# Rows of x and y in DRAM numbered lane by lane, two experts' KAN weights asked for on ScalarE's queue, and some normalised copies written by VectorE

## The chip, the cores and the metric

One core of one Trainium2 chip. The metric is device microseconds for one launch of the whole program. Everything is float32 in DRAM and SBUF unless it is said otherwise. SBUF has 128 partitions, called lanes below.

## The reference, cut to what matters

`x` is 2048 tokens of 128 channels. The program computes three residual steps in a row: a mixture of experts, attention with its own feed-forward part, and the same mixture again.

```python
x = x + 0.5 * ffn(layernorm(x))           # first mixture
x = x + attn(layernorm(x))                # windowed attention, then SiLU-gated ffn
x = x + 0.5 * ffn(layernorm(x))           # second mixture, the same weights

def ffn(x):                               # 8 experts, the best 2 of each token
    w_full = normalised top-2 of softmax(x @ gate_W)
    # experts 0 to 3, MLP:   gelu(x @ W1 + b1) @ W2 + b2        (128 -> 512 -> 128)
    # experts 4 to 7, KAN:   basis(layernorm(x)) @ W0 + b0, layernorm, basis, @ W1 + b1
    #   basis: 8 values 1 - tanh^2((x - grid) / 2) for each channel (1024 -> 256, 2048 -> 128)
    return sum over experts of expert_out * w_full
```

## The kernel before, in words

**Stages.** `macaron` runs `route` and `moe_blocks` for the first mixture (n = 0), then the attention (`project`, `attend`, `finish_attention`), then `route` and `moe_blocks` again (n = 1). Inside each function every engine has its own instruction stream, written by hand in the order in which it runs; there is no scheduler. Streams wait for each other only through semaphores and at the ends of the functions' blocks.

**How x lies.** `k.xs` holds token t*128 + p in lane p, tile t (16 tiles of 128 channels). In `route` two normalised copies of each token are written into `k.got`: `xn` (for the MLP experts) and `xh` (for the KAN experts), both by ScalarE, 32 activations (L560) in four chunks of four tiles. As soon as a chunk is written, the SP queue copies it to `x_rows` in DRAM (L459). There a token's row number is its token number, so one lane's four tiles of a chunk lie 128 rows apart and each goes as a run of 512 bytes.

**Routing.** TensorE transposes x (L501) and multiplies by the gate (L519); VectorE picks the best two experts, counts, and sorts the tokens into blocks of 128 with one expert each (L344 to L438). The numbers that it sorts are in `token_no`. The result is `rows_of`: for each block the rows to read from `x_rows` and the rows to write in `y_rows`. GpSimd waits until all of `x_rows` has landed (`rows_in_dram`) and until `rows_of` is ready, and then starts the first gathers (L480).

**Blocks.** `moe_blocks` gathers 128 rows by an indirect DMA of GpSimd (L692), runs the expert, and scatters the result to `y_rows` (L697). First come MLP blocks in pairs, then two blocks that fill the start of the KAN pipeline, then a joint loop that runs one MLP and one KAN block per round, and a loop for KAN blocks alone. For each MLP block ScalarE copies the expert's W1 out of `k.mlp_w1` into `m_w1` (L1173), because TensorE loads it from a fixed place; TensorE's first product waits for it (`m_w1_ready`, L849). The second product (L858) takes W2 straight from `k.mlp_w2`, hidden channel c*128 + p in lane p, slice c.

**Weights of the first mixture.** All are asked for on the SP queue, in this order: x in four parts, `b1`, W1, four W2 and b2 of the MLPs (`load_mlps`), the shared small tensors (`load_shared`), then the eight writes of `x_rows` as their chunks become ready, then eight loads of 1 MB with the KAN weights (`load_kan`, L199 and L201). `b1` comes as 16 rows that TensorE turns (L524) and ScalarE copies (L552). TensorE waits for all of the KAN weights before the first KAN product (L871).

**The end of each mixture.** When all of `y_rows` is there, they are read back into `got` in eight parts (SP for the first choice, L1255; ScalarE's queue for the second, L1243), again in runs of 512 bytes; ScalarE weighs the second (L572), VectorE adds both to x (L581, L586).

## Time and profile before

| what | value |
|---|---|
| median of 3 runs | 637.17 us (632.69 to 643.67) |
| the profiled execution, its own time | 639.1 us |
| its span from first to last instruction | 637.3 us |
| mean granted TensorE clock | 0.927 of full speed |
| TensorE busy | 558.2 us |
| VectorE, ScalarE, GpSimd busy | 454.3, 401.1, 262.1 us |
| KAN weights, first mixture | 8 loads of 1024 KB on SP's queue |

A row of a timeline tells when a group of instructions of one engine starts (microseconds from the start of the span), how long it takes from the first to the last, the line, what is written from what, and, in square brackets, how long the engine sat idle before it and what ended that. In the program the first mixture ends at about 219 us, the attention at about 420 us, and the second mixture at the end.

### The profile page before, as it was taken

What the parts mean: (1) busy time and instruction counts of PE and PEld (TensorE: products, weight loads), DVE (VectorE), ACT (ScalarE), POOL (GpSimd) and SP (SyncE); (2) the same over time, 40 slices, a digit from 0 to 9 for tenths busy, and PEclk for the clock granted to TensorE, in tenths of its full rate; (3) what the DMA queues carried; (4) which work ended last, traced back from release to release, by engine and by line L of the source; (5) the groups of instructions that cost most, each with busy time, mean ns of one, the idle gap of its engine ahead of it and who ended that gap; (6) DMA issues with size and microseconds to landing.
All of it is one profiled execution on the core that took longest, in us unless ns stands there. A gap on an engine that the chain in (4) does not pass through costs nothing. (4 is left out here: it accounts for less than half of the span.)

```text
span 637.3 us, 19397 instructions
## 1 busy us (share of the span) xinstructions
PE 558.2 (88%) x6514; PEld 494.5 (78%) x6515; DVE 454.3 (71%) x1135; ACT 401.1 (63%) x954; POOL 262.1 (41%) x314
## 2 busy tenths in 40 slices
PE   9677899999999488888889888998788999999970
PEld 8666899999999355766778783688788999999970
DVE  6734768788788576699678788557466787878864
ACT  4645868889875158710456523256587789888943
POOL 7144556555544345820000013221455556656540
PEclk7768989999999869999999999985798999999995
DMA  8793222100101220000100039303111000110106
GB/s 264 246 407 100 67 62 86 45 26 29 33 16 19 68 78 3 4 3 14 16 5 4 5 120 402 156 29 114 34 30 26 25 27 27 33 29 25 29 18 202
DMA packets 41433, 46.58 MB, mean 73 GB/s; under 512 B 7409, under 2 KB 33377, under 8 KB 40353
## 3 DMA queue, kind: packets, MB, share of 16 engines
q1 hardware_dynamic: 32272, 33.99, 15.9%
q0 software_dynamic: 4736, 9.71, 5.5%
q10 hardware_dynamic: 4368, 2.10, 1.1%
q8 instruction: 39, 0.64, 0.4%
q14 instruction: 18, 0.14, 0.1%
HBM read 35.69 MB, written 10.09 MB: 72 GB/s over the span
## 5 line engine op out<-in xcount | busy, mean ns | idle before, releaser
L881 PE MATMUL k_y_ps<-kan_w,k_basis 128*128 x1056 | 128.5, 281 | 7.3 <-DVE k_basis L978 7.3
L881 PEld LDWEIGHTS k_y_ps<-kan_w,k_basis 128*128 128x128 f32 x1056 | 124.4, 196 | 9.6 <-issue 9.2
L871 PE MATMUL k_z_ps<-kan_w,k_basis 128*128 x528 | 120.5, 381 | 0.6 <-issue 0.6
L1151 ACT ACTIVATE k_sig<-k_h1T 128x256 f32<-128x256 f32 x264 | 84.4, 402 | 47.5 <-DVE k_h1T L1005 47.4
L871 PEld LDWEIGHTS k_z_ps<-kan_w,k_basis 128*128 128x128 f32 x528 | 98.2, 191 | 13.3 <-issue 1.1
L978 DVE SCALAR_TENSOR_TENSOR k_basis<-k_sig 128x512 f32<-128x512 f32 x132 | 88.1, 690 | 14.6 <-ACT k_sig L1151 14.6
L1817 ACT ACTIVATE got<-p_ps 128x960 f32<-128x960 f32 (+1 forms) x44 | 39.2, 944 | 42.0 <-PE p_ps L1672 41.9
L1144 ACT ACTIVATE k_sig<-k_h0T 128x128 f32<-128x128 f32 x280 | 59.2, 294 | 7.6 <-DVE k_h0T L966 7.6
L697 POOL DMA_INDIRECT y_rows<-k_y,k_rows x33 | 34.3, 1041 | 53.8 <-DVE j_y L1033 28.3
L849 PE MATMUL m_z_ps<-m_xT,m_w 128*128 128x128 f32 x304 | 43.3, 289 | 8.1 <-ACT m_w L1173 4.9
L849 PEld LDWEIGHTS m_z_ps<-m_xT,m_w 128*128 128x128 f32 x304 | 41.4, 202 | 11.1 <-ACT m_w L1173 6.3
L1743 DVE TENSOR_REDUCE p_minus_max<-p_ps 128x6 f32<-128x960 f32 (+1 forms) x44 | 45.8, 1116 | 4.9 <-PE p_ps L1637 4.4
L704 POOL TENSOR_TENSOR k_rstd<-k_var_eps,minus_half 128x1 f32<-128x1 f32 x33 | 31.7, 961 | 39.8 <-DVE k_var_eps L995 39.7
L972 DVE SCALAR_TENSOR_TENSOR k_basis<-k_sig 128x512 f32<-128x512 f32 x70 | 47.8, 685 | 0.0
L1622 PE MATMUL p_ps<-s_kT,s_q_bd 32*128 32x160 f32 (+3 forms) x864 | 35.2, 303 | 8.7 <-DVE p_minus_max L1743 7.9
L858 PE MATMUL m_y_ps<-mlp_w,m_hT 128*128 x304 | 42.8, 286 | 0.0
L1622 PEld LDWEIGHTS p_ps<-s_kT,s_q_bd 32*128 32x128 f32 x864 | 30.0, 185 | 14.1 <-DVE p_minus_max L1743 13.0
L858 PEld LDWEIGHTS m_y_ps<-mlp_w,m_hT 128*128 128x128 f32 x304 | 39.0, 201 | 0.5 <-issue 0.3
L692 POOL DMA_INDIRECT k_x_in<-x_rows,k_rows x31 | 33.3, 1073 | 10.4 <-issue 8.8
L1173 ACT COPY m_w<-mlp_w 128x512 f32 x40 | 24.8, 620 | 18.0 <-issue 13.3
L1990 POOL TENSOR_TENSOR f_rstd<-f_var_eps,minus_half 128x4 f32<-128x4 f32 x4 | 5.5, 1382 | 69.9 <-DVE f_var_eps L2025 69.9
L692 POOL DMA_INDIRECT j_x_in<-x_rows,j_rows x24 | 25.1, 1046 | 20.8 <-POOL j_rows L795 16.5
(270 smaller groups left out, 1089.5 us busy)
## 6 DMA issues: line engine op xcount, KB each, us to landing
kan_w<-in_L_ffn_kan_sl_W_dram SPq DMA_DIRECT2D x16, 1024.0 KB, 14.0
x_rows<-got SPq DMA_DIRECT2D x16, 256.0 KB, 2.5
mlp_w<-in_L_ffn_mlp_W_dram SPq DMA_DIRECT2D x2, 1024.0 KB, 5.9
mlp_w<-in_L_ffn_mlp_W_dram SPq DMA_DIRECT2D x8, 256.0 KB, 6.7
got<-y_rows SPq DMA_DIRECT2D x8, 256.0 KB, 4.9
got<-y_rows ACTq DMA_DIRECT2D x8, 256.0 KB, 5.4
xs<-in_L_attn_x_dram SPq DMA_DIRECT2D x4, 256.0 KB, 3.8
s_cos<-in_cos_dram SPq DMA_DIRECT2D x8, 128.0 KB
```

The source lines that it names most:

```text
L692: pool.indirect_dma_start(dst[:], None, k.x_rows, bass.IndirectOffsetOnAxis(ap=rows.bitcast(U32), axis=0)).then_inc(landed, 16)
L849: last = nc.tensor.matmul(m_z_ps[:, c], m_w1[:, c * P:(c + 1) * P], m_xT[:], start=True, stop=True)
L858: last = nc.tensor.matmul(m_y_ps, m_hT[:, c], k.mlp_w2[:, bass.ds(e, 1), c], start=(c == 0), stop=(c == FC - 1))
L871: last = nc.tensor.matmul(z_ps, basis0[:, g], k.kan_w0[:, bass.ds(e, 1), g], start=(g == 0), stop=(g == G - 1))
L881: last = nc.tensor.matmul(y_ps, basis1[:, g, c], k.kan_w1[:, bass.ds(e, 1), c, g], start=(g == 0 and c == 0), stop=(g == G - 1 and c == F2 ...
L972: nc.vector.scalar_tensor_tensor(basis0[:, part], sig0[:, part], 1.0, sig0[:, part], ALU.subtract, ALU.mult).then_inc(basis0_ready, 1)
L978: nc.vector.scalar_tensor_tensor(basis1[:, part], sig1[:, part], 1.0, sig1[:, part], ALU.subtract, ALU.mult).then_inc(basis1_ready, 1)
L1144: ins = nc.scalar.activation(sig0[:, g], h0T[:], ACT.Sigmoid, bias=float(-GRID[g]))
L1151: ins = nc.scalar.activation(sig1[:, g], h1T[:], ACT.Sigmoid, bias=float(-GRID[g]))
L1622: nc.tensor.matmul(banks[g][:, i * SPAN + lead:(i + 1) * SPAN], s.q_bd[rows(g), b], s.kT[rows(g), b * QB + lead - WINDOW:(b + 1) * QB], st ...
L1743: nc.vector.tensor_reduce(minus_max[:, h, 2 * half:2 * half + 2, b0:b0 + n], src, AX.X, ALU.max, negate=True).then_inc(reduced, 1)
L1817: nc.scalar.activation(prob[t % 2][:, 2 * half:2 * half + 2, 0:n * SPAN], ps[:, at:end, 0:n * SPAN], ACT.Exp).then_inc(exp_done, 1)
```

## The change

Four things are changed.

1. **Numbering.** The row of a token in `x_rows` and `y_rows` is now lane*16 + tile. `token_no` is made with that number, and the views of the writes to `x_rows` and of the reads from `y_rows` follow it. A lane's four tiles of a chunk are now one run of 2 KB. How x itself is read and the output written is as it was.
2. **MLP weights.** W2 is now loaded with hidden channel p*4 + c in lane p, slice c: one run of 2 KB per lane for each expert. The copy of W1 into `m_w1` puts the columns into that order: it reads contiguously and writes each following element 512 bytes on. `b1` is loaded in that order directly, in runs of 16 bytes; the transpose and the copy of it are gone.
3. **KAN weights.** Experts 0 and 1 (4 MB) are asked for on ScalarE's queue, ahead of ScalarE's normalised copies; experts 2 and 3 stay on SP's queue behind the writes of `x_rows`.
4. **Normalised copies.** VectorE writes `xn` of the first two chunks in the first mixture (8 instructions) and of the first three in the second (12). ScalarE leaves these out.

```diff
-            (k.token_no, [[0, TOPK], [P, NT]], 1, 1), (k.slot_at, [[P, NS]], -P, 0),
+            (k.token_no, [[0, TOPK], [1, NT]], 1, NT), (k.slot_at, [[P, NS]], -P, 0),
...
-        q.dma_start(k.mlp_w2[:, e], a.mlp_W2[e].rearrange("(c p) h -> p c h", p=P)).then_inc(k.mlp_loaded[n], 16)
+        q.dma_start(k.mlp_w2[:, e], a.mlp_W2[e].rearrange("(p c) h -> p c h", p=P)).then_inc(k.mlp_loaded[n], 16)
...
+        ON_VECTOR = 3 if n else 2
...
+                for g in range(ON_VECTOR):
+                    if n == 0:
+                        dve.wait_ge(stats.powered, g + 1)
+                    elif g >= NCH - 2:
+                        dve.wait_ge(stats.powered, g - (NCH - 2) + 1)
+                    for t in range(g * PART, (g + 1) * PART):
+                        last = nc.vector.tensor_scalar(xn[:, t], k.xs[:, t], k.mv[:, t, 0:1], k.scale2[:, t, 0:1],
+                                                       ALU.subtract, ALU.mult)
+                    last.then_inc(xn_ready, 1)
 
                 dve.wait_ge(logits_ready, 1)
...
-                    b1_rows = a.mlp_b1.rearrange("e (c p) -> (e c) p", p=P)
-                    sp.dma_start(b1_rows_sb[:], b1_rows).then_inc(k.b1_loaded, 16)
+                    sp.dma_start(k.mlp_b1[:], a.mlp_b1.rearrange("e (p c) -> p e c", p=P)).then_inc(k.b1_loaded, 16)
...
-                rows = k.x_rows.rearrange("(h t p) c -> h p t c", h=2, p=P)
+                rows = k.x_rows.rearrange("(h p t) c -> h p t c", h=2, p=P)
...
+                    if g < ON_VECTOR:
+                        sp.wait_ge(xn_ready, g + 1)
...
-                    for e in range(E2):
+                    for e in range(2, E2):
                         load_kan(sp, k, a, n, e)
...
-                    pe.wait_ge(k.b1_loaded, 16)
-                    nc.tensor.transpose(b1_ps[:], b1_rows_sb[:], k.ident[0:E2 * FC, 0:E2 * FC]).then_inc(b1_turned, 1)
...
-                    act.wait_ge(b1_turned, 1)
-                    nc.scalar.copy(k.mlp_b1[:].rearrange("p e c -> p (e c)"), b1_ps[:])
+                    for e in range(2):
+                        load_kan(act, k, a, n, e)
...
+                            if x == 0 and g < ON_VECTOR:
+                                continue
...
-        got_rows = k.y_rows[0:TOPK * T].rearrange("(j t p) c -> p j t c", j=TOPK, p=P)
+        got_rows = k.y_rows[0:TOPK * T].rearrange("(j p t) c -> p j t c", j=TOPK, p=P)
...
-                    nc.scalar.copy(m_w1[:], k.mlp_w1[:, bass.ds(e, 1)].rearrange("p o f -> p (o f)")
+                    nc.scalar.copy(m_w1[:].rearrange("p (c q) -> p q c", c=FC),
+                                   k.mlp_w1[:, bass.ds(e, 1)].rearrange("p o (q c) -> p (o q) c", c=FC)
                                    ).then_inc(m_w1_ready, 1)
```

ScalarE's stream in `route` of the first mixture, from its first request to the table load, stands so in the kernel before (`got` is where the normalised copies go, `mlp_b` is b1):

```order
L546 DMA gate_w<-in_L_ffn_gate_W_dram 128x8
L549 ACT_TABLE_LOAD
L549 COPY xT<-xT_ps_0 128x512 x4
L552 COPY mlp_b<-b_ps 128x16
L560 ACTIVATE got<-xs,shift,scale 128x128 x32
L564 ACTIVATE second<-gap 128x16
```

and so in the changed kernel:

```order
L554 DMA gate_w<-in_L_ffn_gate_W_dram 128x8
L557 ACT_TABLE_LOAD
L557 COPY xT<-xT_ps_0 128x512 x4
L199 DMA kan_w_0<-in_L_ffn_kan_sl_W_dram 128x2048
L201 DMA kan_w_0<-in_L_ffn_kan_sl_W_dram 128x2x1024
L199 DMA kan_w_0<-in_L_ffn_kan_sl_W_dram 128x2048
L201 DMA kan_w_0<-in_L_ffn_kan_sl_W_dram 128x2x1024
L570 ACTIVATE got<-xs,shift,scale 128x128 x24
L574 ACTIVATE second<-gap 128x16
```

Four requests of 1 MB stand where one small copy stood, and 8 of the 32 activations are gone.

VectorE's stream in the same place, from the last chunk's statistics to the choice of experts, in the changed kernel (before, the row with `got` isn't there and the others follow each other in the same order):

```order
L221 BN_STATS st<-xs 128x6 x4
L225 BN_AGGR mv<-st 128x2 x4
L228 TENSOR_SCALAR var<-mv 128x4
L229 TENSOR_SCALAR var<-mv 128x4
L230 TENSOR_SCALAR minus_mean<-mv 128x4
L346 TENSOR_SCALAR got<-xs,mv,scale 128x128 x8
L352 TENSOR_REDUCE top<-logit_ps 128x16
L358 TENSOR_TENSOR ties<-logit_ps,top 128x128
```

The eight copies stand ahead of the first instruction that needs the logits.

SP's queue in the first mixture, from b1 to the last KAN load, in the changed kernel:

```order
L458 DMA mlp_b<-in_L_ffn_mlp_b_dram 128x4x4
L192 DMA mlp_w_0<-in_L_ffn_mlp_W_dram 128x4x512
L194 DMA mlp_w_0<-in_L_ffn_mlp_W_dram 128x512 x4
L195 DMA mlp_b_0<-in_L_ffn_mlp_b_dram 128x512
L183 DMA kan_ln<-in_kan_ln_dram 128x24
L184 DMA kan_b<-in_L_ffn_kan_sl_b_dram 128x1024
L185 DMA kan_b<-in_L_ffn_kan_sl_b_dram 128x512
L469 DMA x_rows<-got 128x512 x8
L199 DMA kan_w_0<-in_L_ffn_kan_sl_W_dram 128x2048
L201 DMA kan_w_0<-in_L_ffn_kan_sl_W_dram 128x2x1024
L199 DMA kan_w_0<-in_L_ffn_kan_sl_W_dram 128x2048
L201 DMA kan_w_0<-in_L_ffn_kan_sl_W_dram 128x2x1024
```

Before, the same requests stood there with eight KAN loads behind the writes of `x_rows` in place of four; the writes of `x_rows` and the loads of W2 had the form 128x4x128 (runs of 128 elements) in place of 128x512.

## Rows read from the trace of the kernel before

**Rows 1.** The page, part 1: each engine's busy us, share, instructions.

```profile
PE 558.2 (88%) x6514; PEld 494.5 (78%) x6515; DVE 454.3 (71%) x1135; ACT 401.1 (63%) x954; POOL 262.1 (41%) x314
```

**Rows 2.** Timeline, head of the first mixture: from ScalarE's transposed copy to the gather.

```profile
8.73 0.58 ACT L549 COPY xT<-xT_ps 128x512 f32<-128x512 f32 x1 [0.70 <-PE xT_ps L501]
...
11.60 0.29 DVE L344 TENSOR_REDUCE top<-logit_ps 128x16 f32<-128x128 f32 x1 [1.39 <-PE logit_ps L519]
...
11.89 12.43 ACT L560 ACTIVATE got<-xs,shift,scale 128x128 f32<-128x128 f32 x32
...
26.24 0.21 DVE L417 SCALAR_TENSOR_TENSOR rows_of<-token,kan_rows 128x48 int32<-128x48 f32 x1
...
28.52 1.20 POOL L480 DMA_INDIRECT m_x_in<-x_rows,rows_of  x1 [12.16 <-DMA x_rows<-got]
```

**Rows 3.** Windows: engines' busy us, then granted clock, DMA share, GB/s.

```profile
2.50:15.00 12.50, 12.43 (x72) 11.88 (x71) 9.11 (x55) 5.52 (x14) 8.98 (x13) 0.76 1.07 325
15.00:25.50 10.50, 7.06 (x59) 6.41 (x59) 9.51 (x37) 10.48 (x27) 1.36 (x3) 0.83 0.58 167
28.50:49.70 21.20, 15.06 (x83) 12.72 (x81) 6.96 (x20) 7.55 (x18) 9.84 (x10) 0.74 1.01 401
377.00:379.00 2.00, 2.00 (x20) 2.00 (x20) 1.90 (x11) 0.00 (x0) 0.37 (x1) 1.00 1.03 376
380.00:384.00 4.00, 3.21 (x27) 2.78 (x26) 3.90 (x18) 0.36 (x1) 1.40 (x2) 1.00 1.16 324
386.00:402.00 16.00, 14.35 (x60) 7.77 (x59) 11.05 (x32) 5.76 (x9) 4.36 (x3) 1.00 1.02 417
```

**Rows 4.** DMA issues, median us to landing: 30 to 40 us, then 425 to 450.

```profile
m_x_in<-x_rows,rows_of POOLq DMA_INDIRECT x3, 5.8
...
m_x_in<-x_rows,rows_of POOLq DMA_INDIRECT x3, 2.5
```

**Rows 5.** Timeline of TensorE, first mixture: first turn, third MLP product, first KAN product.

```profile
34.51 0.47 PE L843 MATMUL m_xT_ps<-ident,m_x_in 128*128 128x128 f32 x1 [0.69 <-DMA m_x_in<-x_rows,rows_of]
...
43.32 1.06 PE L849 MATMUL m_z_ps<-m_xT,m_w 128*128 128x128 f32 x8
...
55.28 4.42 PE L871 MATMUL k_z_ps<-kan_w,k_basis 128*128 x16
```

**Rows 6.** Timeline of TensorE, second mixture: the same three places.

```profile
449.09 0.36 PE L843 MATMUL m_xT_ps<-ident,m_x_in 128*128 128x128 f32 x1
...
456.24 1.06 PE L849 MATMUL m_z_ps<-m_xT,m_w 128*128 128x128 f32 x8
...
464.86 3.72 PE L871 MATMUL k_z_ps<-kan_w,k_basis 128*128 x16 [0.57 <-issue]
```

**Rows 7.** Groups by form, and two single lines: durations (ns min/median/max).

```profile
L1173 ACT COPY m_w<-mlp_w 128x512 f32 x40 | 24.8, 620 | 18.0 <-issue 13.3 <-PE m_xT_ps L843 4.7
...
L430 DVE TENSOR_REDUCE tab<-passed x2: 472/472/473, 27.7 to 442.5; 128x96 f32<-128x288 f32 x2
...
L427 DVE TENSOR_TENSOR passed<-slot_at,rows_up_to x2: 449/450/451, 27.1 to 441.9; 128x288 f32<-128x288 f32 x2
```

**Rows 8.** ScalarE in one joint round; then the waits: total us, times, longest.

```profile
515.04 2.56 ACT L1151 ACTIVATE k_sig<-k_h1T 128x256 f32<-128x256 f32 x8 [0.82 <-DVE k_h1T L1005]
...
PEld m_z_ps L849 <- ACT m_w L1173: 6.3, 4, 2.7
```

**Rows 9.** Timeline, end of the second mixture: read-back and adding.

```profile
623.22 2.13 ACTq L1243 DMA_DIRECT2D got<-y_rows  x4
...
627.11 1.28 ACT L572 ACTIVATE got<-got,weight 128x128 f32<-128x128 f32 x4 [10.33 <-DMA got<-y_rows]
...
629.09 1.13 DVE L581 SCALAR_TENSOR_TENSOR xs<-got,weight,xs 128x128 f32<-128x128 f32 x4
```

**Rows 10.** Timeline of VectorE: four normalising instructions; the second mixture's wait for logits.

```profile
388.23 1.11 DVE L2008 TENSOR_SCALAR f_n<-s_res,f_mv,f_rstd 128x128 f32<-128x128 f32 x4
...
426.44 0.29 DVE L344 TENSOR_REDUCE top<-logit_ps 128x16 f32<-128x128 f32 x1 [3.98 <-PE logit_ps L519]
```

More of the change, by code:

```diff
@@ L299, in route @@
         found_ps = [ps(f"found_ps{j}", [P, 4 * P])[:, 0:NS] for j in range(TOPK)]
-        b1_ps = ps("b1_ps", [P, E2 * FC]) if n == 0 else None
-        b1_turned = sem("b1_turned")
-        b1_rows_sb = sb("b1_rows", [E2 * FC, P])
         gate_summed, gate_ready, last_added = sem("gate_summed"), sem("gate_ready"), sem("last_added")
@@ L308, in route @@
         sums_ready, counts_ready = sem("sums_ready"), sem("counts_ready")
-        normed, rows_ready = sem("normed"), sem("rows_ready")
+        normed, xn_ready, rows_ready = sem("normed"), sem("xn_ready"), sem("rows_ready")
         found_ready = sem("found_ready")
@@ L440, in _ @@
                     dve.wait_ge(k.small_loaded, 16 * N_SHARED)
+                    dve.wait_ge(k.b1_loaded, 16)
             @block.sync
```

## The prediction

> **What bounds the kernel now.** I read the engines' busy shares first. TensorE is busy for 558 of 637 us [rows 1]; the joint loops of both mixtures keep it full, and nothing in this change takes a product away from them. Time can only be won where TensorE waits, so I looked next at the timelines of the stages that the change touches: the head of the first mixture, its MLP pairs, the copy into `m_w1`, and the reading back of `y_rows`. In the head, GpSimd sits idle for 12.16 us until all of `x_rows` has landed and starts the first gather at 28.52; `rows_of` was ready at 26.24 + 0.21 = 26.45 [rows 2]. So ScalarE's 32 copies (11.89 to 24.32) and their writes end last there, about 2 us behind VectorE's sorting. Then the reader should see a second, larger cost: the first mixture takes 55.28 − 34.51 = 20.77 us from the first turn to the first KAN product [rows 5], the second takes 464.86 − 449.09 = 15.77 us for the same work [rows 6]. The difference of 5.0 us is the time in which the KAN weights fill the DMA engines: from 28.5 to 49.7 they are full at 401 GB/s [rows 3], and a gather then takes 5.8 us to land in place of 2.5 [rows 4].
>
> **The change, part by part.**
>
> *Start of the gathers.* ScalarE is free after its last transposed copy at 9.31 [rows 2]. Four requests on a queue (about 0.5 us each by the spacing of the 4 requests of got, 2.13 us in rows 9) fill the time to 11.4, so its copies start at about 11.5, near the 11.89 of before. A copy costs 12.43 / 32 = 0.39 us; 24 of them end at 11.5 + 9.3 = 20.8 in place of 24.3. If their writes were free to go, `x_rows` would be complete near 23.5. They are not. Until 15 us the queue of SP moves 325 GB/s [rows 3]: by 11 us that is 8.5 us × 325 = 2.8 MB of the 4.2 MB that stand ahead of the writes (x 1.05, MLP weights 2.36, shared 0.80). SP's queue then still has 1.4 + 2.1 = 3.5 MB to move, and ScalarE's queue has 4.2 MB of KAN weights beside it. With equal shares of some 380 GB/s, SP's part is done at 11 + 3.5 / 0.19 = 29.5; if the long runs of the KAN weights get three quarters, they end at 25 and SP's part at about 30.7; if SP's queue were served first, it would be done by 23.5. That a gather of short rows beside the KAN weights lands in 5.8 us in place of 2.5 [rows 4] speaks for a queue of short runs getting the smaller part. I take 30.0 for the landing of `x_rows`, against 28.5 now: the gathers start 1.7 us later, the first turn comes at 36.2.
>
> The Trainium skill ("DMA: Bandwidth & Descriptors", section "Queues, rings and completion order") says that each DMA engine takes turns between the queues that have work, one packet each, and in its rules for kernel authors that spreading DMAs over several queues brings no bandwidth. By it the KAN weights on ScalarE's queue go ahead of writes that the old order served first; the rows of the gathers agree, and it is what the rival "the writes are crowded out" rests on.
>
> *End of the KAN weights.* The engines moved only 167 GB/s between 15 and 25.5 [rows 3]; the change fills this gap. After 11 us there are 3.5 MB of SP's and 8.4 MB of KAN weights. Runs of 512 bytes go at 324 GB/s, of 2 KB at 376, of the KAN weights at 417 [rows 3]. At 350 and 410 GB/s this is 10.0 + 20.5 us, with the few gathers an end at about 42.5 in place of 49.7.
>
> *The MLP pairs.* I split the stretch at the third MLP product. Before it: 43.32 − 34.51 = 8.81 us in the first mixture, 7.15 in the second; behind it: 11.96 and 8.62 [rows 5, 6]. With the first turn at 36.2 the third product comes at 45.0, after the weights have landed, so the first piece keeps its 8.8 us and the second costs 8.62: first KAN product at 53.6 in place of 55.28. **Gain 1.7 us.**
>
> *VectorE's copies.* Four instructions of this kind with two scalars per lane take 1.11 us [rows 10], so 8 take 2.2 and 12 take 3.3 us. In the first mixture VectorE waits only 1.39 us for the logits [rows 2]: its chain moves by 0.85 us, and `rows_of` to 27.3. The later landing of `x_rows` covers this; without that cover it costs 0.85. In the second mixture the wait is 3.98 us [rows 10] and covers all of it. There ScalarE's copies aren't what the gathers wait for, so nothing is gained either.
>
> *b1.* A transpose and a small copy go, both beside other work: nothing. The load in runs of 16 bytes stands ahead of the MLP weights on SP's queue. No row shows one; it moves 8 KB and I bound it by nothing and by 1 us on the landing of `x_rows`, and take it as inside the 30.0.
>
> *Copy into `m_w1`.* 40 instructions of 620 ns [rows 7] now write each element 512 bytes from the last. No row has such a write. The nearest is VectorE's reduction that reads 288 elements 192 bytes apart in 472 ns, beside 450 for 288 contiguous ones [rows 7]: nearly free. The bounds are 620 ns and three times that. In a joint round the copy is followed by 0.82 us of idle ScalarE [rows 8], so 24 of the 40 cost nothing until the copy takes over 1.44 us. Of the other 16, TensorE waits for about 4 (6.3 us in 4 waits, [rows 8]), so each 0.1 us there costs 0.4. I take 0.03 us more: **loss 0.1 us.**
>
> The Trainium skill ("SBUF — State Buffer", section "Door 1: The DMA port swizzle", its note on cachelines) says the opposite: SBUF has lines of 16 bytes, full rate needs two accesses to a line, and float32 elements further apart pay. VectorE's row doesn't show that penalty for reads; no row here tests a write. By the page, the copy would be slower, as in the third rival.
>
> *Reading back.* Runs of 2 KB at 376 in place of 324 to 346 GB/s. The first part lands 3.9 us after its request [rows 9], of which 0.5 MB are 1.5 us: 0.15 us less. After it VectorE's adding sets the pace: 629.09 − 627.11 is 2.0 us for a part, more than the 1.5 us that a part takes to arrive. So 0.15 us for each of two mixtures: **gain 0.3 us.**
>
> *Sum.* −1.7 + 0.1 − 0.3 = −1.9 us. The profiled execution took 639.1 us, so 637.2 for one like it. The median of the runs is 1.9 us below the profiled one: 637.2 − 1.9 = 635.3 us.
>
> **The rivals.**
>
> *The writes get through* (faster, −4.3). If `x_rows` lands by 27, the gathers start at 27.6, when `rows_of` is ready, and the first turn is at 33.6. First piece 8.8, second 8.6 and 0.2 for gathers that still meet the weights: KAN product at 51.2, a gain of 4.1, with the read-back and the copy −4.3: 632.9 us. For it: the writes are 2 KB runs now and come in four portions. Against it: the 5.8 us of the gathers.
>
> *The writes are crowded out* (no change). `x_rows` lands at 32, with b1's short runs ahead of everything. First turn at 38.2, the third product at 46.6, KAN product at 55.2: the early weights give back what the late start takes. 637 us.
>
> *The strided copy is slow* (slower). At 1.24 us (twice) 4 waits cost 0.62 each, 2.5 us, and the sum is +0.5: 637.7. From 1.44 us on every joint round pays. At 1.86 us: 24 × (1.86 − 1.44) = 10.1, the pairs 4 to 8 × 1.24 = 5 to 10, minus 1.9: +13 to +18, 650 to 655 us. Against it stands only VectorE's row, a read; for it the page.
>
> *The numbering does nothing for the runs.* Then the 0.3 and part of the 1.7 are missing: 636. The rows at 324 and 376 GB/s make this unlikely; it lies inside the range. Gathered rows now lie 8 KB apart or more in place of 512 bytes to 2 KB. No row shows what this does; it would show first in the landing of gathers, 2.5 us now where nothing else runs [rows 4].
>
> **How the numbers follow.** My forecast 0.48; writes get through 0.16; crowded out 0.20; strided copy up to 1.44 us 0.09; above it 0.07. The single runs of before spread by 5 us to both sides, so 635.3 stands with that noise around it: the likeliest case alone gives 630 to 640. The range goes from 629.0, which takes in the faster rival with some of the noise, to 642.0, which takes in the crowded case and the copy at twice its time, and leaves out the heavy copy. 2% is 12.7 us (about what a measurement of this kernel can tell from no change): 624.4 and 649.9. Nothing above reaches the lower one but noise, 0.03. The upper one needs the heavy copy: 0.06. Within 2%: 0.91.
>
> **What would show it.** In the changed kernel's profile: ScalarE's copies end near 21; the wait of GpSimd's first gather ends with the landing of `x_rows` at 29 to 31; DMA between 15 and 25.5 near 370 GB/s and quiet from about 42.5; the first KAN product at 53 to 54; the m_w1 group at 620 to 700 ns; 8 copies of VectorE of 2.2 us ahead of the logits' first use, which moves to 12.4. I am wrong if the gathers start before 27.5 or after 32, if the m_w1 copy takes over 0.9 us, or if the joint round, the distance of two k_sig groups, is no longer the same.

## The result and the profile after

| | before | after |
|---|---|---|
| median of 21 runs each | 634.77 us (630.4 to 643.67) | 637.64 us (636.28 to 644.9) |
| ratio after / before | | 1.0063, 95% interval 1.0039 to 1.0087 |
| profiled execution | 639.1 us | 637.25 us |
| its span, mean granted clock of TensorE | 637.3 us, 0.927 | 635.4 us, 0.942 |

The change makes the kernel slower by 0.4 to 0.9%, about 4.0 us; I had forecast 1.9 us less. Every ratio in this document is formed from the fast executions alone (before has some over 1.5% above its fastest), so it is not the quotient of the two medians, which here lie 2.9 us apart. The time itself, 637.64 us, lies in the range that I gave, but that is no merit: the range stood on a median of before of 637.17 us from three executions, and with 634.77 the same forecast would have read 632.9 us. The sign is wrong. The two profiled executions must not be compared by their spans: the one of before is 4.3 us above the median of before now known. It lost most of this in the joint rounds: from the first KAN product to the first request of `got` it took 218.73 − 55.28 = 163.45 us, where the changed kernel and all kernels of the experiments take 160.1 to 161.4. What can be compared is each place with a cause of its own.

I call the parts of the change by these numbers below: **part 1** the numbering of the rows, **part 2** the hidden units of the MLPs by lane (W2, `b1` and the copy into `m_w1`), **part 3** two experts' KAN loads on ScalarE's queue at the head, **part 4** VectorE's normalised copies.

The head of the first mixture, timeline of the changed kernel (start, duration, engine, line, what it writes and reads, how often; in brackets the idle time before and what ended it), beside [rows 2]:

```profile
8.70 0.34 ACTq L199 DMA_DIRECT2D kan_w<-in_L_ffn_kan_sl_W_dram  x1
...
10.02 2.18 DVE L346 TENSOR_SCALAR got<-xs,mv,scale 128x128 f32<-128x128 f32 x8
...
10.71 9.34 ACT L570 ACTIVATE got<-xs,shift,scale 128x128 f32<-128x128 f32 x24 [1.43 <-issue]
12.11 0.28 DVE L352 TENSOR_REDUCE top<-logit_ps 128x16 f32<-128x128 f32 x1
12.38 9.70 SPq L469 DMA_DIRECT2D x_rows<-got  x8
...
22.13 1.60 SPq L199 DMA_DIRECT2D kan_w<-in_L_ffn_kan_sl_W_dram  x1
...
26.91 0.21 DVE L425 SCALAR_TENSOR_TENSOR rows_of<-token,kan_rows 128x48 int32<-128x48 f32 x1
...
35.37 1.20 POOL L490 DMA_INDIRECT m_x_in<-x_rows,rows_of  x1 [19.03 <-DMA x_rows<-got]
```

ScalarE's copies end at 20.05 in place of 24.3, `rows_of` is ready at 27.1, and then GpSimd waits until 35.37 for rows that were asked to be written by 22.1. The gathers start 6.85 us later than before. The requests say where the time went; DMA issues, 8 to 40 us, changed kernel (count, KB each, median us from request to landing):

```profile
kan_w<-in_L_ffn_kan_sl_W_dram ACTq DMA_DIRECT2D x4, 1024.0 KB, 14.3
...
x_rows<-got SPq DMA_DIRECT2D x8, 256.0 KB, 13.8
...
kan_b<-in_L_ffn_kan_sl_b_dram SPq DMA_DIRECT2D x1, 256.0 KB, 17.6
```

A write of `x_rows` takes 13.8 us (median) to land; before, it took 2.5. What each queue moved between 15 and 27 us (packets, MB, share of 16 engines; q10 is ScalarE's queue, q1 SP's):

```profile
q10 hardware_dynamic: 725, 3.47, 69.8%
...
q1 hardware_dynamic: 768, 1.48, 32.0%
```

The two queues get nearly the same number of packets, 725 and 768, but those of the KAN weights are 4.8 KB in the mean and those of SP 1.9 KB. So ScalarE's queue moves 289 GB/s, and the queue on which everything waits 123. e2 below, whose writes go in runs of 512 bytes, shows it more sharply: from 15 to 20 us the queues get 359 and 357 packets and move 1.83 and 0.18 MB. The windows beside [rows 3] (engines' busy us, then granted clock, DMA share, GB/s):

```profile
15.00:25.50 10.50, 7.86 (x51) 7.27 (x52) 9.43 (x33) 6.44 (x16) 1.34 (x3) 0.79 1.02 413
25.00:35.20 10.20, 4.98 (x32) 4.78 (x31) 3.94 (x24) 0.00 (x0) 0.00 (x0) 0.73 1.04 325
35.30:43.30 8.00, 5.20 (x21) 4.57 (x22) 0.57 (x2) 1.16 (x3) 4.04 (x4) 0.50 0.97 387
43.30:47.00 3.70, 2.37 (x11) 1.97 (x10) 2.22 (x5) 3.51 (x10) 1.89 (x2) 0.50 0.33 108
```

The gap of 167 GB/s before 25.5 us is filled, and the engines' load falls off after 43.3 us in place of 49.7. The very last of the KAN loads lands at 44.9 us (asked for at 24.89, 20.0 us to landing), before it was 50.4 (29.55 and 20.8). TensorE's places, to be read beside [rows 5]:

```profile
41.40 0.47 PE L853 MATMUL m_xT_ps<-ident,m_x_in 128*128 128x128 f32 x1 [0.48 <-DMA m_x_in<-x_rows,rows_of]
...
50.10 1.10 PE L859 MATMUL m_z_ps<-m_xT,m_w 128*128 128x128 f32 x8
...
59.30 3.07 PE L881 MATMUL k_z_ps<-kan_w,k_basis 128*128 x13 [0.62 <-issue]
```

The first turn comes 6.9 us later than before, the first KAN product 4.0 us later. The stretch between them has shrunk from 20.77 to 17.90 us.

The copy into `m_w1` beside [rows 7], as a group (busy us, mean ns of one, idle before), in the waits (total us, times, longest) and in one joint round, to be read beside [rows 8]:

```profile
L1183 ACT COPY m_w<-mlp_w 128x512 f32 x40 | 43.7, 1092 | 30.9 <-issue 26.4 <-PE m_xT_ps L853 4.5
...
PE m_z_ps L859 <- ACT m_w L1183: 6.9, 6, 1.8
...
512.11 2.56 ACT L1161 ACTIVATE k_sig<-k_h1T 128x256 f32<-128x256 f32 x8 [0.34 <-DVE k_h1T L1015]
```

The same wait in the kernel before:

```profile
PE m_z_ps L849 <- ACT m_w L1173: 4.9, 3, 2.5
```

In the joint round ScalarE's idle time falls from 0.82 to 0.34 us, by what the copy has grown, and the next such group starts 9.25 us later in both kernels.

And the end of the second mixture beside [rows 9]:

```profile
620.25 1.93 SPq L1266 DMA_DIRECT2D got<-y_rows  x4
...
624.89 1.28 ACT L582 ACTIVATE got<-got,weight 128x128 f32<-128x128 f32 x4 [11.07 <-DMA got<-y_rows]
...
631.96 0.69 DVE L596 TENSOR_TENSOR xs<-xs,got 128x512 f32<-128x512 f32 x1
```

The first part lands 4.64 us after its request (3.90 before), and the last addition starts 11.71 us after it; before it was 10.60.

### The profile page after: what moved, and what is told of

Same layout as the page of the kernel before. It is cut to its first block and busy times, and to the rows that moved or that the text cites. A ratio compares the mean times of both kernels' runs of the same rounds, so it can differ in the third digit from the quotient of the medians.

```text
span 635.4 us, 19400 instructions
## 1 busy us (share of the span) xinstructions
PE 549.5 (86%) x6513; PEld 488.4 (77%) x6514; DVE 459.3 (72%) x1155; ACT 410.2 (65%) x933; POOL 264.8 (42%) x314
## 5 line engine op out<-in xcount | busy, mean ns | idle before, releaser
L891 PE MATMUL k_y_ps<-kan_w,k_basis 128*128 x1056 | 126.8, 278 | 6.5 <-DVE k_basis L988 6.5
L891 PEld LDWEIGHTS k_y_ps<-kan_w,k_basis 128*128 128x128 f32 x1056 | 122.8, 194 | 8.8 <-issue 8.5
L1183 ACT COPY m_w<-mlp_w 128x512 f32 x40 | 43.7, 1092 | 30.9 <-issue 26.4
L1633 PE MATMUL p_ps<-s_kT,s_q_bd 32*128 32x160 f32 (+3 forms) x864 | 35.2, 303 | 8.7 <-DVE p_minus_max L1754 7.9
L702 POOL DMA_INDIRECT j_x_in<-x_rows,j_rows x24 | 25.1, 1047 | 20.8 <-POOL j_rows L805 15.6
```

Of the source, the lines that this page charges most:

```text
L702: pool.indirect_dma_start(dst[:], None, k.x_rows, bass.IndirectOffsetOnAxis(ap=rows.bitcast(U32), axis=0)).then_inc(landed, 16)
L891: last = nc.tensor.matmul(y_ps, basis1[:, g, c], k.kan_w1[:, bass.ds(e, 1), c, g], start=(g == 0 and c == 0), stop=(g == G - 1 and c == F2 ...
L1183: nc.scalar.copy(m_w1[:].rearrange("p (c q) -> p q c", c=FC), k.mlp_w1[:, bass.ds(e, 1)].rearrange("p o (q c) -> p (o q) c", c=FC)).then_i ...
L1633: nc.tensor.matmul(banks[g][:, i * SPAN + lead:(i + 1) * SPAN], s.q_bd[rows(g), b], s.kT[rows(g), b * QB + lead - WINDOW:(b + 1) * QB], st ...
```

## The experiments

The theories of the first round: Q, the loads on ScalarE's queue crowd SP's out; C, the slow copy into `m_w1` costs time; R, runs of 2 KB that lie 8 KB apart are read slowly; V, fewer copies on ScalarE pay of themselves. The medians are this kernel's / that of before on the same chip in the same rounds; kernels of different chips are compared by their ratios. "Gathers" is the start of GpSimd's first gather, "KAN" the first KAN product, "end" the time from the first request of `got` at the end of the second mixture to the start of the last addition.

| kernel | parts in it | ratio, 95% interval | medians, us | gathers | KAN | end |
|---|---|---|---|---|---|---|
| before | none | 1 | | 28.52 | 55.28 | 10.60 |
| after | 1 2 3 4 | 1.0063, 1.0039 to 1.0087 | 637.64 / 634.77 | 35.37 | 59.30 | 11.71 |
| e1 | 1 2 4 | 0.9954, 0.9923 to 0.9985 | 635.09 / 637.99 | 28.04 | 53.62 | 11.95 |
| e2 | 3 | 1.0064, 1.0030 to 1.0097 | 641.57 / 637.99 | 34.67 | 58.87 | 10.37 |
| e3 | 1 3 4 | 1.0077, 1.0041 to 1.0114 | 642.75 / 637.99 | 34.90 | 58.84 | 11.65 |
| e4 | 2 3 4 | 1.0016, 0.9983 to 1.0050 | 640.51 / 637.99 | 33.98 | 59.90 | 10.62 |
| e5 | 4 | 0.9963, 0.9923 to 1.0004 | 630.49 / 635.03 | 28.09 | 52.73 | 10.39 |
| e6 | 4, one expert ahead on SP | 0.9967, 0.9926 to 1.0008 | 631.06 / 635.03 | 30.25 | 54.56 | 10.36 |
| e9 | 1 2 4, one expert ahead on SP | 1.0025, 0.9991 to 1.0060 | 634.26 / 635.03 | 29.19 | 52.96 | 11.79 |
| e10 | 1 2 4, two experts ahead on SP | 1.0093, 1.0056 to 1.0131 | 639.10 / 635.03 | 34.37 | 59.11 | 11.81 |
| e7 | 1 2 4, copy read by steps | 0.9993, 0.9959 to 1.0027 | 634.53 / 636.78 | 30.08 | 54.76 | 11.91 |
| e8 | 1 | 1.0028, 0.9989 to 1.0066 | 637.77 / 636.78 | 30.28 | 58.25 | 11.85 |
| e11 | 2 4 | 0.9951, 0.9917 to 0.9984 | 632.02 / 636.78 | 27.81 | 53.97 | 10.40 |
| e12 | 4, once more | 0.9942, 0.9906 to 0.9978 | 633.82 / 636.78 | 27.83 | 53.87 | 10.50 |
| e13 | 4, numbering without gaps | 0.9928, 0.9895 to 0.9962 | 633.40 / 637.73 | 27.79 | 52.10 | 10.14 |

### Part 3 undone, and part 3 alone

e1 is the changed kernel with all KAN loads on SP, behind the writes of `x_rows`:

```diff
-                    for e in range(2):
-                        load_kan(act, k, a, n, e)
...
-                    for e in range(2, E2):
+                    for e in range(E2):
                         load_kan(sp, k, a, n, e)
```

> The changed kernel with all eight KAN loads back on SP's queue, behind the writes of x_rows. Theory Q (the loads on ScalarE's queue crowd out what SP's queue still holds, and that is the loss): the first gather of the first mixture starts at 28 to 29 in place of 35.4, held by rows_of (27.1) and not by the writes; the first KAN product comes at 55 to 56 in place of 59.3; the time is 3 to 5 us below the changed kernel, a ratio to the kernel before of 0.998 to 1.002. Theory C (the slow copy into m_w1 is the loss): nothing of that, a ratio of 1.005 or more as in the changed kernel, the KAN product still 3 us or more later than before. Theory R (runs of 2 KB 8 KB apart are slow, in the writes too): the writes of x_rows land over 4 us after their request with nothing beside them, and the gather starts after 30.

e2 is the kernel before with this part alone:

```diff
                 if n == 0:
+                    for e in range(2):
+                        load_kan(act, k, a, n, e)
                     act.wait_ge(b1_turned, 1)
...
-                    for e in range(E2):
+                    for e in range(2, E2):
                         load_kan(sp, k, a, n, e)
```

> The kernel before with one edit: experts 0 and 1 are asked for on ScalarE's queue after its transposed copies. Theory Q: x_rows is complete at 33 to 37 although its runs are 512 bytes as before, the first KAN product comes at 58 to 60, the time is 3 to 5 us above the kernel before (ratio 1.005 to 1.008). Theories C and R: the copy and the runs are the old ones, so at most 1 us (ratio below 1.002). If the earlier end of the KAN weights (49.7 before, about 43 here) were worth more than the late start, the ratio would be below 1.

With the part undone, GpSimd's first gather starts at 28.04 us and is no longer held by the writes; timeline of e1:

```profile
28.04 1.25 POOL L490 DMA_INDIRECT m_x_in<-x_rows,rows_of  x1 [11.71 <-DVE k_rows_first L432]
```

The time falls from 1.0063 to 0.9954 of before. Alone, the part costs 1.0064, all that the whole change costs. Theory Q holds.

### Queue or bytes

Is it the second queue, or that 4.2 MB are asked for ahead of the writes? e10 has no second queue: the two experts' weights stand on SP, behind the shared tensors and ahead of the writes. e9 has one expert there, and e6 has one expert there on the kernel before with part 4.

```diff
                     load_shared(sp, k, a)
+                    for e in range(2):
+                        load_kan(sp, k, a, n, e)
```

> The changed kernel with the same two experts' KAN weights ahead of the writes of x_rows, but on SP's queue in place of ScalarE's. It tells the queue from the bytes. Bytes: 10.5 MB stand ahead of the end of the writes in both, so x_rows lands at 31 to 35 here too and the ratio is 1.003 to 1.008. Queue (two queues taking turns, in which the long runs win and the small ones are drawn out): with one queue x_rows lands at 30 or before, kan_b and with it the end of the stage near 18, and the ratio is below 1.001.

> The changed kernel with one expert's KAN weights ahead of the writes of x_rows on SP's queue and three behind, none on ScalarE's. Against the kernel with all eight loads behind the writes (0.9954) it fills the DMA engines between 15 and 21 us. Theory Q: the gather stays at 28, the weights land 2 us earlier: ratio 0.992 to 0.996. If the runs of 2 KB make the writes of x_rows late (theory R), the gather starts at 29 to 31 and the ratio is 0.996 to 1.000.

> The kernel before with part 4, and one expert's KAN weights (2.1 MB) asked for on SP's queue ahead of the writes of x_rows, the other three behind. Theory Q as a matter of bytes: 4.2 + 2.1 + 2.1 MB at 360 to 390 GB/s put the landing of x_rows at 25 to 27, still ahead of rows_of (27.3), so the gather starts at 28; all KAN weights are there near 44, the first KAN product at 52 to 53.5: ratio 0.993 to 0.997. If anything ahead of the writes hurts, the gather starts after 29 and the ratio is 0.998 or more.

Timeline of e10, the same instruction:

```profile
34.37 1.20 POOL L492 DMA_INDIRECT m_x_in<-x_rows,rows_of  x1 [17.78 <-DMA x_rows<-got]
```

The start is the same as with the second queue to 1.0 us, and the ratio is 1.0093. So it is the bytes ahead of the writes that cost; the second queue only decides who else is late. On SP, `kan_b` lands 6.4 and 7.4 us after its request, beside the second queue 10.6 and 17.6. One expert ahead (2.1 MB) delays the gathers by 1.2 us (e9 against e1) to 2.2 us (e6 against e5), and nothing comes back for it: e6 and e5 agree in time (0.9967, 0.9963), and e9 is not below e1 (1.0025, 0.9954). Why e9 stands above e1 isn't shown; in the profiled executions its first KAN product comes 0.7 us earlier than e1's. No version gained by asking for any of them earlier.

### Part 2 undone; the copy the other way round

e3 is the changed kernel with the old layout of the hidden units and the old way of `b1`:

```diff
-                    nc.scalar.copy(m_w1[:].rearrange("p (c q) -> p q c", c=FC),
-                                   k.mlp_w1[:, bass.ds(e, 1)].rearrange("p o (q c) -> p (o q) c", c=FC)
+                    nc.scalar.copy(m_w1[:], k.mlp_w1[:, bass.ds(e, 1)].rearrange("p o f -> p (o f)")
```

> The changed kernel with the MLP weights as before: W2 in runs of 512 bytes, the contiguous copy into m_w1 (620 ns in place of 1092), b1 through the transpose. Theory C: the copy is waited for by TensorE at about 4 places of each mixture, so 8 times 0.47 us = 3.8 us at most come back, ratio to before 1.000 to 1.003. Theory Q: only what the waits show (6.9 us against 4.9 us on TensorE): 1 to 2 us come back, ratio 1.003 to 1.006. If the joint rounds had paid, 24 times 0.47 = 11 us would come back; the equal distance of the stages in both profiles speaks against it.

The copy is back at 619 ns, and the time is not lower: 1.0077 against 1.0063. The comparison without part 3 says the same: e11 (parts 2 and 4) is at 0.9951, e5 and e12 (part 4) at 0.9963 and 0.9942. One thing in part 2 works the other way, and I had overlooked it: in the old way ScalarE waits for the turned b1 before it starts its normalised copies. In the kernel before this is 2.51 us of idle time; in e1 the copies start at once:

```profile
11.82 0.17 ACT L552 COPY mlp_b<-b_ps 128x16 f32<-128x16 f32 x1 [2.51 <-PE b_ps L524]
...
9.37 9.34 ACT L569 ACTIVATE got<-xs,shift,scale 128x128 f32<-128x128 f32 x24
```

The first line is of before, the second of e1. In e5, e12 and e13 the copies start at 10.65, 12.08 and 11.85 us, in e1 and e11 at 9.37 and 9.31. So between e11 and e5 or e12 a gain by b1 and a loss by the slow copy could cancel. With part 3 in, ScalarE's four requests fill that wait (the copies start at 10.71 in the changed kernel and at 10.37 in e3), and there the old way is no faster either. Theory C falls as far as these intervals reach, some 2 us: the copy takes 472 ns more, and no time is seen for it. In e7 (on e1) the copy writes in order and reads 16 bytes apart:

```diff
-                    nc.scalar.copy(m_w1[:].rearrange("p (c q) -> p q c", c=FC),
-                                   k.mlp_w1[:, bass.ds(e, 1)].rearrange("p o (q c) -> p (o q) c", c=FC)
+                    nc.scalar.copy(m_w1[:].rearrange("p (c q) -> p c q", c=FC),
+                                   k.mlp_w1[:, bass.ds(e, 1)].rearrange("p o (q c) -> p (o c) q", c=FC)
```

> The changed kernel with part 3 undone (all KAN loads on SP behind the row writes) and the m_w1 copy iterated the other way: it writes each partition's 512 float32 in order and reads them 16 bytes apart, where the changed kernel reads in order and writes 512 bytes apart (1092 ns against 620 ns for in order on both sides). If the scattered write is what ScalarE pays for, the copy falls back to about 620 ns; if any step between elements costs it, read or write, it stays at about 1090; if reads by a step of 16 bytes cost more than that, it rises. In time theory C (the copy's length matters) expects up to 0.47 us per pair on the pair's path at the head, in all some 1 to 2 us below the same kernel with the slow copy, whose ratio to before was 0.9954; the theory that the copy lies under the joint rounds' slack of 0.82 us expects the same 0.995 to 0.996. TensorE's wait for the copy at the first products tells it directly: 6.9 us in 40 with the slow copy, 4.9 with the old one.

Group of e7:

```profile
L1182 ACT COPY m_w<-mlp_w 128x512 f32 x40 | 45.0, 1124 | 26.5 <-issue 22.3 <-PE m_xT_ps L852 4.1
```

1124 ns: ScalarE pays for the step on either side. The ratio, 0.9993, is above that of e1 by 0.4%, but the intervals overlap. Its profiled gathers start 2.0 us later than e1's because `rows_of` is ready 2.0 us later, and that begins with the logits, which VectorE gets at 14.35 us in place of 12.11:

```profile
14.35 0.29 DVE L352 TENSOR_REDUCE top<-logit_ps 128x16 f32<-128x128 f32 x1 [2.15 <-PE logit_ps L529]
```

TensorE's transposes of x took 421 ns each there (median), in e1 306. The profiled executions of e4 and e10 have the same late head (logits at 14.34 and 14.52 us), so it belongs to the execution and not to an edit; why it comes isn't shown. I draw nothing from e7's time. A difference of 2 us or less in "gathers" may be read only between executions whose logits come together, as in e1 and e9 (12.11 and 12.08 us), e5 and e6 (12.16 and 12.10), before and e8 (11.60 and 11.65).

### Part 1: the distance of the runs

e4 is the changed kernel with the old numbering, e8 the kernel before with the new one. The edit of e8 (e4 makes the same one backwards, from the changed kernel):

```diff
-            (k.token_no, [[0, TOPK], [P, NT]], 1, 1),
+            (k.token_no, [[0, TOPK], [1, NT]], 1, NT),
...
-                rows = k.x_rows.rearrange("(h t p) c -> h p t c", h=2, p=P)
+                rows = k.x_rows.rearrange("(h p t) c -> h p t c", h=2, p=P)
...
-        got_rows = k.y_rows[0:TOPK * T].rearrange("(j t p) c -> p j t c", j=TOPK, p=P)
+        got_rows = k.y_rows[0:TOPK * T].rearrange("(j p t) c -> p j t c", j=TOPK, p=P)
```

> The changed kernel with the rows of x and y numbered by token as before (runs of 512 bytes, one contiguous piece of 256 KB for each request). Theory R: the first part of got lands 3.9 us after its request in place of 4.3 and 4.6, so 0.4 and 0.7 us come back at the two ends of mixtures; if the writes of x_rows are slow for the same reason, the first gather starts 1 to 3 us earlier too: ratio to before 1.001 to 1.005. Theory Q: the gather stays at 34 to 36 because the bytes are the same, and only the 1.1 us at the ends come back: ratio 1.004 to 1.005.

> The kernel before with part 1 alone, the numbering by lane (2 KB runs in x_rows and y_rows). The theory of the prediction (2 KB runs read faster, 0.15 us gained at each read-back) expects 0.9995. Theory R (runs of 2 KB that lie 8 KB apart start slowly) expects each read-back's first part at 4.3 to 4.7 us after its request in place of 3.9 to 4.0, and the time 0.7 to 3 us up: 1.001 to 1.005, by what undoing it gave. The start of the gathers should stand at 28.5 us in either, since no KAN load lies ahead of the writes; if it moves by over 0.5 us the writes themselves go slower in the new order, which neither theory has.

The last column of the table splits without overlap: 10.36 to 10.62 us in the seven kernels with the old numbering, 11.65 to 11.95 us in the seven with the new one. (e13 has a third numbering and is told of below.) The means are 10.46 and 11.81, 1.3 us apart. At the first mixture's read-back other work lies between, and the same stretch comes in two lengths; in the shorter it is 20.09 and 20.21 us with the old numbering (e11, e4), 20.49 to 20.71 with the new one (after, e3, e8, e10), 0.4 us apart; in the longer it is 21.51 to 23.08 and 22.36 to 23.10, which overlap, with the means 0.6 us apart. That makes 1.7 us together. The intervals of the ratios can't show this for one pair; of three pairs that differ in part 1 alone, the new numbering is above the old by 0.0028 (e8, before), 0.0003 (e1, e11) and 0.0047 (after, e4), in the mean 0.0026, 1.7 us. e8 adds a place that was not on my list: the last write of `x_rows` lands late and the gathers start at 30.28 in place of 28.52. While it is under way (26 to 28, 28 to 30 us) DMA moves 247 and 324 GB/s, before 293 and 373.

A run of 2 KB in the new numbering is followed by a gap: a request covers four tiles of a lane, 2 KB, and the next lane's begin 8 KB further on. e13 has a third numbering, row 512 g + 4 p + t for part g, on the kernel before with part 4: the same 2 KB runs, one right behind the other.

```diff
-            (k.token_no, [[0, TOPK], [P, NT]], 1, 1),
+            (k.token_no, [[0, TOPK], [P * PART, NT // PART], [1, PART]], 1, PART),
...
+                rows = k.x_rows.rearrange("(h g p t) c -> h g p t c", h=2, p=P, t=PART)
...
+        got_rows = k.y_rows[0:TOPK * T].rearrange("(j g p t) c -> g p j t c", j=TOPK, p=P, t=PART)
```

> The kernel before with part 4, and a third numbering: row = 512 g + 4 p + t for lane p and tile t of part g. A lane's four rows of a part still make one run of 2 KB, as in part 1 of the change, but the runs of a part now follow each other without gaps; in the change they lie 8 KB apart, and in the kernel before the runs are 512 bytes without gaps. Of the read-back at the end, from the request of got on SP to VectorE's last addition, the kernels with 512-byte runs without gaps show 10.4 to 10.6 us, the kernels with 2 KB runs 8 KB apart 11.6 to 11.9 us. If the pitch costs it, this kernel shows 10.5 or less, landings of got of 4.8 us on SP and 5.3 us on ScalarE's queue or less (the prediction's rate for 2 KB runs gives 0.15 us less than the 512-byte runs, 10.3), and the time is that of part 4 alone, ratio 0.994 to 0.996. If the longer runs themselves start slowly, it shows 11.7 us, landings of 6.0 and 6.8, and 0.996 to 0.999.

Windows of half a microsecond at the end of the second mixture (GB/s is the last number), first e8, with the runs 8 KB apart, from 3 us after the first request of `got` on:

```profile
623.60:624.10 0.50, 0.00 (x0) 0.00 (x0) 0.00 (x0) 0.00 (x0) 0.00 (x0) 0.50 0.76 139
624.10:624.60 0.50, 0.00 (x0) 0.00 (x0) 0.00 (x0) 0.00 (x0) 0.00 (x0) 0.50 0.60 119
624.60:625.10 0.50, 0.00 (x0) 0.00 (x0) 0.00 (x0) 0.00 (x0) 0.00 (x0) 0.50 0.82 180
```

e12, runs of 512 bytes without gaps, also from 3 us after the request on:

```profile
622.80:623.30 0.50, 0.00 (x0) 0.00 (x0) 0.00 (x0) 0.00 (x0) 0.00 (x0) 0.50 1.16 349
623.30:623.80 0.50, 0.00 (x0) 0.00 (x0) 0.24 (x1) 0.24 (x1) 0.00 (x0) 0.50 1.15 347
```

e13, runs of 2 KB without gaps, from 2.5 us after the request on:

```profile
616.10:616.60 0.50, 0.00 (x0) 0.00 (x0) 0.00 (x0) 0.00 (x0) 0.00 (x0) 0.50 1.07 410
616.60:617.10 0.50, 0.00 (x0) 0.00 (x0) 0.10 (x1) 0.10 (x1) 0.00 (x0) 0.50 1.05 406
```

Timeline of e13, the same read-back:

```profile
613.58 1.75 SPq L1270 DMA_DIRECT2D got<-y_rows  x4
...
617.00 2.63 ACT L587 ACTIVATE got<-got,weight 128x128 f32<-128x128 f32 x8 [9.85 <-DMA got<-y_rows]
```

The length of the runs was right and their distance was not: 406 to 410 GB/s without gaps, 119 to 180 with them. Whether any gap does it or this distance of 8 KB, no run tells. The first part lands 3.42 us after its request in place of 3.8 to 3.9, and the end takes 10.14 us. The median landings of a request of `got` on SP and on ScalarE's queue are, in the first mixture, 4.4 and 4.9 us here, 5.0 and 5.5 in e12, 6.0 and 6.8 in e8 and in the changed kernel; in the second they are the same within 0.2 us. The writes follow: 2.1, 2.3 and 2.6 us in the second mixture.

### Part 4, and what is best

e5 is the kernel before with part 4, e12 the same once more on another chip, e11 has part 2 as well:

```diff
+                for g in range(ON_VECTOR):
...
+                    for t in range(g * PART, (g + 1) * PART):
+                        last = nc.vector.tensor_scalar(xn[:, t], k.xs[:, t], k.mv[:, t, 0:1], k.scale2[:, t, 0:1],
+                                                       ALU.subtract, ALU.mult)
+                    last.then_inc(xn_ready, 1)
```

> The kernel before with part 4 alone: VectorE writes xn of two chunks (three in the second mixture). Theory V (ScalarE's copies ended last, so taking 8 away is what pays in the first run of experiments): x_rows is complete near 25, rows_of is ready near 27.3 and now ends last, the first gather starts at 27.6 to 28.2 against 28.5, and the KAN loads start 3 us earlier, so the first KAN product comes at 53 to 54 against 55.3: ratio 0.995 to 0.998. Rival L (the gain of the kernel with all KAN loads on SP came from the layout of rows and weights): ratio 0.999 to 1.001.

> The kernel before with part 4 alone, once more on another chip and beside the three kernels above: it stood at 0.9963 with an interval that reached 1.0004. If the gain of some 2.3 us is real, it stands at 0.995 to 0.998 again with a gather start near 28.1 us and the first KAN product near 52.7 us; if it was the day's spread, it stands at 1.000. By the prediction's own sum (ScalarE's copies were not on the path to the gathers) the gain should be nothing.

> The changed kernel with parts 1 and 3 undone: parts 2 and 4 are left, all KAN loads stand on SP behind the row writes. With part 1 in, this stood at 0.9954 to before; with part 4 alone 0.9963. Theory R (numbering costs 0.7 us or more at the two read-backs) expects 0.9930 to 0.9945 here; the theory that the numbering is worth nothing either way expects 0.9954. The theory that part 2 is worth nothing expects that this and part 4 alone agree within their intervals; if the slow m_w1 copy costs time after all, this stands above part 4 alone by 1 to 2 us.

e5 alone left it open whether there is a gain (its interval reaches 1.0004); with e12 (0.9942, 0.9906 to 0.9978) and e11 (0.9951, 0.9917 to 0.9984) it is there, some 3 us. Timeline of e5:

```profile
12.87 8.55 SPq L472 DMA_DIRECT2D x_rows<-got  x8
...
21.46 0.51 SPq L199 DMA_DIRECT2D kan_w<-in_L_ffn_kan_sl_W_dram  x1
...
28.09 1.26 POOL L493 DMA_INDIRECT m_x_in<-x_rows,rows_of  x1 [11.70 <-DVE k_rows_first L435]
...
47.97 0.20 ACT L1172 ACTIVATE m_rows<-rows_of 128x2 int32<-128x2 int32 x1 [1.89 <-DMA y_rows<-m_y,m_rows]
```

The same places in the kernel before:

```profile
15.10 10.15 SPq L459 DMA_DIRECT2D x_rows<-got  x8
...
50.38 0.20 ACT L1157 ACTIVATE m_rows<-rows_of 128x2 int32<-128x2 int32 x1 [3.88 <-DMA y_rows<-m_y,m_rows]
```

The gathers start only 0.4 us earlier. But SP asks for the KAN weights when the last write is on its way, at 21.46 in place of 25.29, and so the last of them lands 4 us earlier, at 46.3 us in place of 50.4. The store of `y_rows`, a transfer of short rows beside them, holds ScalarE's `m_rows` for 1.89 us in place of 3.88 (in e12 still for 3.03), and the first KAN product comes at 52.7 (e5), 53.9 (e12) and 52.1 us (e13) in place of 55.28. That the earlier weights are the cause is read from these places; no run moves them alone. It has a limit, too: in e1 and e11, without the wait for b1, SP asks at 19.63 us and the engines' load falls off by 44 us, some 2 us before e5, and yet the first KAN product comes at 53.6 and 54.0 and the time is no lower.

e13 has the lowest ratio, 0.9928 of before (0.9895 to 0.9962), and is clearly ahead of the changed kernel. Its interval overlaps those of part 4 alone (0.9963 and 0.9942), so the gain of the third numbering in the whole time is not shown, only that in the read-back.

## Why the prediction was wrong

**Start of the gathers: the failed step.** `x_rows` was to land at 30.0 us; GpSimd's wait for it ended at 35.37, and the first turn came at 41.40 in place of 36.2: 5.2 us of the error arise here. That is outside the 29 to 31 us that I named as a sign of being right, and beyond the 32 that I named as a sign of being wrong; the copy into `m_w1`, over 0.9 us, is another such sign. The rival "crowded out" had the right mechanism but 32 us, and so no change in time. Two numbers under it were off. I gave SP's queue half of 380 GB/s or, in the other case, a quarter, 95 GB/s until 25 us; it got 123 between 15 and 27 us. Then I let it run at full rate, but once ScalarE's queue was empty the engines moved 331 GB/s (27 to 30 us) and 231 (30 to 33 us), both below my 350 and the second below the 324 of [rows 3] as well. The writes to rows 8 KB apart may be a part of that: in the same 3 us from 30 on, e2 and e4, without them, move 331 and 335. But e3 and e10, with them, move 348 and 323, and their gathers start within 1 us of those of e2 and e4 (34.90 and 34.37 us beside 34.67 and 33.98), so it is not the main part. The bytes were not 3.5 MB either: SP's queue moved 4.67 MB between 11 and 35.2 us. The 1.2 MB above my count can only be KAN weights that SP asked for from 22.13 on: they were moved before the last of the writes had landed. I had treated a queue as one line. That some of the 16 engines ran ahead of others in it is my reading; no row shows the single engines. e10, with one queue, has the same late landing. The Trainium skill ("DMA: Bandwidth & Descriptors", section "Queues, rings and completion order") has the queues take turns packet by packet: 725 and 768 packets in 12 us agree, as do 359 and 357 in e2, and the bytes then go by the size of the packets.

**End of the KAN weights: nearly right.** The load falls off at 43.3 us and the last one lands at 44.9, 42.5 forecast; 413 GB/s between 15 and 25.5, 370 forecast. Nothing hangs on the difference, since the third product comes at 50.10.

**The MLP pairs: right in size, in the wrong place.** From the first turn to the third product 8.70 us (8.8 forecast), from there to the first KAN product 9.20 (8.62). The stretch did shrink by 2.9 us. It could not pay for a start that was 6.9 us late: 41.40 + 8.70 + 9.20 = 59.30.

**VectorE's copies: the cost right, a gain missed.** 2.18 us in the first mixture and `rows_of` at 27.12 (27.3 forecast). In the second, 12 of them took 3.16 us and the wait for the logits fell from 3.98 to 0.48 us: covered. I wrote that ScalarE's earlier end gains nothing there, and in the first mixture I followed it only to the gathers. It also sets when SP gets to the KAN loads, and that is, as far as the places show it, what the 3 us of e5, e12 and e11 come from. With part 3 in, it is gone: the writes then wait for their queue and no longer for the copies. The change as a whole (1.0063) costs what part 3 costs alone (1.0064).

**b1: a wait read wrongly.** I wrote that the transpose and the copy of b1 lie beside other work. They did not: ScalarE stood idle for 2.51 us until b1 was turned, and only then started the normalised copies. In the changed kernel the four requests take that time, which is why my start of the copies (11.5 us forecast, 10.71 measured) came out close; in the whole time no run shows a gain, e1 and e11 among them.

**The copy into `m_w1`: mis-sized, and without effect.** 1.09 us where I took 0.65; the waits of TensorE for it grew from 4.9 us in 3 to 6.9 us in 6. The copy stays under 1.44 us, so the joint rounds hide it, as [rows 8] said they would: 461.89 to 620.25 is 158.36 us, before it was 158.35. Here the row that I went by, VectorE's read at steps of 192 bytes beside a contiguous instruction of another kind, misled me, and the page that I set beside it, the Trainium skill ("SBUF — State Buffer", section "Door 1: The DMA port swizzle"), was right in direction for ScalarE on both sides, read and write.

**Reading back: the wrong sign.** −0.3 us forecast, +1.7 us measured by rows. The step that failed is the rate: 376 GB/s was measured on 2 KB runs elsewhere in the kernel, and I carried it over by the length of the run alone. Without gaps it holds and more (e13); 8 KB apart the stretch that everything waits for runs at 119 to 307 GB/s. I had named that distance for the gathers only, where it does nothing that can be seen (median landing of the four gathers of the second mixture: 2.7 us before and after).

In all: the first KAN product came 59.30 − 53.6 = 5.7 us later than forecast, the reading back cost 2.0 us more than forecast, and the copy 0.1 less. With −1.9 that makes +5.7 us; 4.0 were measured, and the interval reaches to 5.5. The first number rests on one execution of each kernel, and places like it differ by over 1 us between executions of one kernel (first KAN product of e5 and e12, 52.73 and 53.87).

What stays open: why gaps of 6 KB between runs make DRAM so slow at first and not later (from 626 to 628 us, some 6 us after the first request, the changed kernel moves 404 GB/s), whether a distance other than 8 KB would do the same, and where the 231 GB/s at 30 to 33 us comes from, which e3 with the same numbering doesn't show.

## What to carry to other kernels

Filling an idle stretch of the DMA engines is no gain of itself: list what must land before the path can go on, and ask for nothing large ahead of it, on no queue; bytes asked for earlier are bytes ahead of it. The other way about, an engine that writes small tiles may be worth relieving even where nobody waits for it, if large loads stand behind its writes. Read what an engine waits for right before the stage, too: a transpose of 16 rows, behind the logits in TensorE's stream, held ScalarE for 2.51 us, and I had priced it at nothing. And with layouts in DRAM take both numbers, the length of a run and the distance to the next run of the same request; runs that follow each other without gaps gave all that longer runs had promised.

## What the runs showed of the hardware

- Two queues with work shared the engines by packets, 725 to 768 between 15 and 27 us, not by bytes, 3.47 to 1.48 MB; with runs of 512 bytes in the one queue (e2, 15 to 20 us) 359 to 357 packets were 1.83 to 0.18 MB.
- 256 KB requests of 2 KB runs 8 KB apart: between 2 and 5 us after the first request 119 to 307 GB/s (e8 and the changed kernel), landing in 6.0 and 6.8 us (median, two queues at once); 512-byte runs without gaps (e12, from 3 us on): 344 to 349 GB/s, 5.0 and 5.5 us; 2 KB runs without gaps (e13, from 2 us on): 373 to 418 GB/s, 4.4 and 4.9 us.
- ScalarE's float32 copy of 512 elements per lane: 620 ns in order, 1092 ns when it writes 512 bytes apart, 1124 ns when it reads 16 bytes apart. VectorE's reduction that reads 288 elements 192 bytes apart took 5% longer than a contiguous instruction of another kind on as many [rows 7].
